# Order of the hand-over work between an expert mixture and a state-space layer, one power instruction, and squares made beside a sort

## The reference, cut to what matters

```python
# first mixture: top 2 of 8 experts, 256 hidden units
for e in range(n_experts):
    h = jax.nn.gelu(tokens @ w1[e].T, approximate=False)
    out = out + gate[:, e:e + 1] * (h @ w2[e].T)
...
# state-space layer, behind a layer norm and an RMS norm
u = h @ Win + b_in                       # 128 -> 256 channels
u = causal_conv(u, conv_w, taps=4) + conv_b
hc = einsum('bdr,drs->bds', hc, A) + u_t[:, :, None] * Bv[None]   # 16 states a channel, A is 16x16
y = einsum('bds,ds->bd', hc, Cv)
return y @ Wout + b_out + res
```

## Time and profile before

| | before |
|---|---|
| median of 3 runs | 1023.79 us (1021.31 to 1026.02) |
| the profiled execution, its own time | 1022.04 us |
| its span in the trace | 1020.2 us |
| mean granted clock of TensorE | 0.923 of 2.4 GHz |
| busy: PE / DVE / ACT / POOL | 867.4 / 540.7 / 453.2 / 462.6 us |
| attention with its sorts ends, first copy of the ticks | 380.06 us |
| tick 1 begins on PE | 390.23 us |
| squares of the last tick done, turning for the scan begins | 606.21 us |

### The profile page before, as it was taken

How to read it: one execution, slowest core, us unless ns; L and a number is a source line. 1 busy time by engine, 2 the same in 40 slices (tenths; PEclk the granted TensorE clock), 3 DMA queues, 4 the chain that set the end, 5 groups by cost and what they waited for, 6 DMA issues and landing times. The chain is left out here.

```text
span 1020.2 us, 25008 instructions
## 1 busy us (share of the span) xinstructions
PE 867.4 (85%) x9254; PEld 730.8 (72%) x9254; DVE 540.7 (53%) x1574; ACT 453.2 (44%) x991; POOL 462.6 (45%) x491
## 2 busy tenths in 40 slices
PE   4999999999998509977777469999977999999991
PEld 2777777777776508966666349999876679999991
DVE  4666657666576534444555557446376823222225
ACT  5545445454443004535554457442414453444443
POOL 3234353444444464655544410015503277677764
PEclk9999999999999758979888769999997999999995
DMA  7676700000000013322221110000014023322245
GB/s 251 232 282 266 300 23 8 13 16 8 18 13 17 22 45 83 106 75 74 65 66 28 42 21 4 3 4 2 1 31 180 17 73 80 88 81 89 86 114 165
DMA packets 72148, 78.78 MB, mean 77 GB/s; under 512 B 14285, under 2 KB 55892, under 8 KB 71536
## 3 DMA queue, kind: packets, MB, share of 16 engines
q1 hardware_dynamic: 61024, 59.02, 18.4%
q0 software_dynamic: 9152, 16.84, 4.8%
q10 hardware_dynamic: 1872, 1.58, 0.5%
HBM read 31.79 MB, written 47.64 MB: 78 GB/s over the span
## 5 line engine op out<-in xcount | busy, mean ns | idle before, releaser
L1733 POOL DMA_INDIRECT mixed<-ssm_H,ssm_target x78 | 77.4, 992 | 97.1 <-DVE ssm_H L2214 82.3
L449 POOL TENSOR_TENSOR attn_qd<-attn_qT,attn_qpow 128x512 f32<-128x512 f32 x32 | 51.3, 1602 | 130.5 <-DVE attn_qT L775 130.5
L1335 ACT ACTIVATE routed_hT<-routed_hid,routed_B 128x256 f32<-128x256 f32 x160 | 65.8, 471 | 81.0 <-PE routed_hid L1258 81.0
L1176 POOL DMA_INDIRECT results<-routed_outs,routed_target x80 | 78.5, 981 | 30.5 <-issue 16.5
L1161 POOL DMA_INDIRECT queue_in<-routed_XN,routed_slot x64 | 63.7, 995 | 45.3 <-DVE routed_slot L1436 22.3
L1270 PE MATMUL routed_outp<-routed_W,routed_hT 128*128 128x128 f32 x640 | 77.8, 275 | 0.0
L1258 PE MATMUL routed_hid<-routed_cols,routed_W 128*128 128x256 f32 x320 | 75.8, 380 | 0.5 <-DVE routed_cols L1484 0.5
L1270 PEld LDWEIGHTS routed_outp<-routed_W,routed_hT 128*128 128x128 f32 x640 | 74.7, 192 | 0.1
L439 POOL DMA_INDIRECT sorted_rows<-attn_sent_rows,attn_slot x56 | 57.2, 1022 | 18.3 <-issue 14.3
L1258 PEld LDWEIGHTS routed_hid<-routed_cols,routed_W 128*128 128x128 f32 x320 | 57.7, 190 | 6.9 <-ACT routed_shared L1314 0.7
L1824 PE MATMUL ssm_pb<-powers_XB,powers_XC 64*64 64x65 f32 (+4 forms) x640 | 31.8, 244 | 35.2 <-ACT powers_XC L2057 24.2
(11 more groups left out here) (339 smaller groups left out, 2263.1 us busy)
## 6 DMA issues: line engine op xcount, KB each, us to landing
sorted_rows<-attn_vacant SPq DMA_DIRECT2D x8, 2080.0 KB, 8.7
queue_in<-attn_empty SPq DMA_DIRECT2D x8, 645.0 KB, 7.2
routed_rows<-queue_in SPq DMA_DIRECT2D x40, 129.0 KB, 2.3
ssm_H<-sorted_rows SPq DMA_DIRECT2D x39, 130.0 KB, 2.1
results<-attn_zero SPq DMA_DIRECT2D x8, 512.0 KB, 8.2
ssm_turn_buf<-mixed SPq DMA_DIRECT2D x16, 256.0 KB, 3.3
routed_W<-m1w SPq DMA_DIRECT2D x2, 2048.0 KB, 10.2
xs<-x SPq DMA_DIRECT2D x8, 256.0 KB, 4.2
```

The source lines that it names most:

```text
L449: pool.tensor_tensor(wide(of_pair(qd, p)), wide(of_pair(qT, p)), qpow[:, p * P:(p + 1) * P].unsqueeze(1).to_broadcast([P, BATCH, P]), ALU. ...
L1176: pool.indirect_dma_start(results, bass.IndirectOffsetOnAxis(target[:, n:n + 1], 0), outs[t % KEPT_BACK][:, j * P:(j + 1) * P], None, boun ...
L1335: last = act.activation(hT[t % 2][:, m * GROUP:(m + 1) * GROUP], banks[q % 4][:, (m % 2) * GROUP:(m % 2 + 1) * GROUP], ACT.Silu, bias=B1[: ...
L1733: pool.indirect_dma_start(results, bass.IndirectOffsetOnAxis(target[:, 2 * q + j:2 * q + j + 1], 0), outs[q][:, j * P:(j + 1) * P], None, ...
```

## The change

**The tick table.** Every link of the hand-over chain gets a tick of its own, and some run at the start of a tick's body where they ran at its end:

| step | before | after |
|---|---|---|
| SP fetch back | 18, end | 17, end |
| POOL add (`mixed`) | 15, end | 14, end |
| DVE add and statistics (`mixed`, `stated`) | 16, end | 16, end |
| POOL powers | 16, end | 17, start |
| DVE shift (`scaled_means`) | 17, end | 18, start |
| ACT tokens | 17, end (ahead of the copies of squares) | 19, end |
| PE columns | 18, end | 20, start |
| PE input products | 19 and 20, end | 20 and 21, end |
| ACT columns, channels | 19; 20 and 21 | 20; 21 and 22 (ahead of the first weights) |
| DVE taps | 22, 23, 24 | 22, 23, 24 |

**One power.** Both variances stand side by side in one buffer, and POOL's two powers are one instruction of 128 x 2 x 4.

**The ring of rows.** It has 5 buffers (was 4). The tags are no longer copied: `kept_of` reads them from the rows, and a buffer is given back to SP only after it.

**The squares.** They move to a class that both phases use. 22 of the 40 sets are made at the end of the attention phase, in the banks of scores and products that are free by then, two pairs in turn: 5 sets ahead of the last chunk's `rows_turned`, 3 between its `logits_of` and `counted`, 14 behind `counted`. The other 18 follow on ticks 34 to 51, one a tick, with one pair of banks.

```diff
-            pool.tensor_tensor(of.both[:, tiles], of.wide_var[:, tiles], of.mhalf[:, tiles], ALU.pow)
-            front.power(pool, c, tiles)
+            pool.wait_ge(front.moments, at(c, 7, 7))
+            pool.tensor_tensor(of.pair(of.inverse, tiles), of.pair(of.spreads, tiles), of.pair(of.mhalves, tiles), ALU.pow
+                               ).then_inc(front.rstd_ready, 1)
...
+            def squares_kept(begin, end):
+                for m in range(begin, end):
+                    squares.kept(act, m, *squares_at(m))
...
             spread(LAST - 1)
+            squares_kept(0, SQUARED_FIRST[0])
             rows_of(LAST)
             sorted_columns(LAST)
+            squares_kept(SQUARED_FIRST[0], SQUARED_FIRST[1])
             spread(LAST)
+            squares_kept(SQUARED_FIRST[1], SQUARED_FIRST[2])
...
+            squares_of(0, SQUARED_FIRST[0])
             rows_turned(LAST)
             logits_of(LAST, proj[1])
+            squares_of(SQUARED_FIRST[0], SQUARED_FIRST[1])
             pe.wait_ge(s["put"], at(LAST - 1, PLACED, SUMS_READ))
             counted(LAST, proj[0])
+            squares_of(SQUARED_FIRST[1], SQUARED_FIRST[2])
...
+SQUARED_FIRST = (5, 8, 22)
...
-        FETCHED_BACK, MIXED, STATED, SCALED, TURNED, INPUT, KEPT_IN, CONVOLVED = 18, 15, 16, 17, 18, 19, 20, 22
+        FETCHED_BACK, MIXED, STATED, ROOTED, SCALED, TURNED, INPUT, CONVOLVED = 17, 14, 16, 17, 19, 20, 20, 22
...
+        LATE = TICKS - 1 - (NSQUARES - SQUARED_FIRST[-1])
...
             for t in range(TICKS):
+                if due(t, TURNED) is not None:
+                    columns(due(t, TURNED))
...
-                if t < NSQUARES:
-                    squares(t)
+                if squares_due(t) is not None:
+                    squares.multiplied(pe, squares_due(t), squares_b, squares_c, turns=1)
...
             def columns_of(n):
-                if n >= BODY:
-                    dve.wait_ge(s["outs"], n - 1)
                 dve.tensor_copy(cols[n % 2], turn).then_inc(s["cols"], 1)
-                dve.tensor_copy(tag4[:, n % BODY], by_row(rows[n % BODY])[:, :, D:TAGGED]).then_inc(s["rows_read"], 1)
...
                 kept.then_inc(s["outs"], 1)
+                dve.wait_ge(s["outs"], n + 3)
+                dve.sem_inc(s["rows_read"], 1)
```

More of the change, by code:

```diff
@@ L179, in attention_phase @@
                     queue, results, coming, sorting, table, sorted_rows, router, rank, before,
-                    powers):
+                    powers, squares):
     with ExitStack() as ctx:
@@ L619, in outputs_turned, with squares_of @@
                 mm.then_inc(s["ytr"], 1)
+            def squares_of(begin, end):
+                pe.wait_ge(s["zeroed"], 11)
+                for m in range(begin, end):
+                    squares.multiplied(pe, m, *squares_at(m), turns=2)
             def combined(i):
@@ L1591, in first_vectors, with __init__, multiplied, kept @@
             pool.tensor_copy(row[:, :, 0:1], table[:, :, STATES:STATES + 1])
-def mixed_space_phase(nc, xs, of, W1, W2, table, sorted_rows, powers, scratch, results):
+class Squares:
+    def __init__(self, S, powers):
+        self.b3, self.c3 = powers.b3, powers.c3
+        self.product, self.copied = (S.sem(n) for n in "product copied".split())
+    def multiplied(self, pe, m, bank_b, bank_c, turns):
+        k, q = divmod(m, NT)
+        n = 2 ** k
+        if m >= turns:
+            pe.wait_ge(self.copied, m - turns + 1)
+        for left, right, bank in ((self.c3, self.b3, bank_b), (self.b3, self.c3, bank_c)):
+            for k_, g in enumerate(range(SETS[q].start, SETS[q].stop)):
+                for part in ROWS:
+                    mm = pe.matmul(bank[part, k_ * (n + HALF):(k_ + 1) * (n + HALF)], left[part, g, n:n + HALF],
+                                   right[part, g, 0:n + HALF], start=True, stop=True)
+        mm.then_inc(self.product, 1)
+    def kept(self, act, m, bank_b, bank_c):
+        k, q = divmod(m, NT)
+        n = 2 ** k
+        act.wait_ge(self.product, m + 1)
+        act.activation(self.b3[:, SETS[q], n:2 * n + HALF], wide(bank_b[:, 0:SET * (n + HALF)], SET), ACT.Copy)
+        src = wide(bank_c[:, 0:SET * (n + HALF)], SET)
+        if k < LEVELS - 1:
+            act.activation(self.c3[:, SETS[q], n:2 * n + HALF], src, ACT.Copy).then_inc(self.copied, 1)
+        else:
+            act.activation(self.c3[:, SETS[q], n:2 * n], src[:, :, 0:n], ACT.Copy)
+            act.activation(self.c3[:, SETS[q], REACH + 1:REACH + 1 + HALF], src[:, :, n:n + HALF], ACT.Copy
+                           ).then_inc(self.copied, 1)
+SQUARED_FIRST = (5, 8, 22)
+def mixed_space_phase(nc, xs, of, W1, W2, table, sorted_rows, powers, squares, scratch, results):
     with ExitStack() as ctx:
@@ L1612, in lent @@
             return H[:, cut[0] - width:cut[0]]
-        rows = [lent(2 * TAGGED) for _ in range(BODY)]
+        rows = [lent(2 * TAGGED) for _ in range(RING)]
         cols, w1, w2 = ([lent(GROUP) for _ in range(2)] for _ in range(3))
@@ L1812, in output_of @@
                 mm.then_inc(s["outp"], 1)
[L1814 to L1820, removed]
-                for left, right, bank in ((c3, b3, squares_b), (b3, c3, squares_c)):
-                    for k_, g in enumerate(range(SETS[q].start, SETS[q].stop)):
-                        for part in ROWS:
-                            mm = pe.matmul(bank[part, k_ * (n + HALF):(k_ + 1) * (n + HALF)], left[part, g, n:n + HALF],
-                                           right[part, g, 0:n + HALF], start=True, stop=True)
-                mm.then_inc(s["lev_mm"], 1)
             def columns(i):
@@ L2318, in build @@
             sorting = Sorting(Scope(nc, until_spaced, "sorting"))
+            squares = Squares(Scope(nc, until_spaced, "squares"), powers)
             with ExitStack() as until_mixed:
```

101 lines of the change are left out of this document (48 added, 53 removed).

## The result

The changed kernel takes 969.94 us (968.15 to 974.8), against 1022.55 on the same chip; the ratio is 0.949, 95% interval 0.944 to 0.954. A second set of runs, beside the experiments, gave 974.09 against 1019.25: 0.954 (0.951 to 0.957).

What follows compares the result with a forecast made beforehand. PE bounds the ticks, standing 7.02 us in hand-over periods for ACT's copies of squares behind a POOL-DVE-ACT chain. From 1022.04, -1.3 + 17.4 + 28.3 + 5.5 - 16.6 = 33.3 saved: 989 us, range 972 to 1006.

Steps and rivals of the forecast that it cites:

- POOL sends at its floor: Ticks 1 to 13: POOL's two sends of 0.97, each behind 0.30 of issue, set 2.54 us a tick, 33.0 in all.
- the sort hides the 22 sets: Last sort: sets fit in PE's idle time at full clock; 1.3 us taken as cost, bounds -3 to +14.
- the periods: Ticks 18 to 33, four ticks with a hand-over each: 16.5 us a period, before 22.7; 28.3 saved in all.
- the price of the tail: From tick 39 on: 13 sets, PE and ACT in turns; 40 to some 58 us, 49 taken, 16.6 lost.
- ticks 34 to 38: Squares are back on these ticks: 5 x 3.2 + 2.9 + 3.8 = 22.7 us, before 28.2; 5.5 saved.
- wait of 3.8: PE's wait in a hand-over for DVE's tick of 6.0 us against PE's 2.12; also counted in ticks 34 to 38.
- Tags read from the rows save DVE a copy per tick: Ticks: tags uncopied, SP's buffer back two ticks later, fetch still two ticks ahead with five buffers; effect nothing.
- A: Rival, chance 0.22: hand-over wait stays and moves to PE's columns; periods 18.4 plus 1.8 per hand-over, 999 to 1000 us.
- B: Rival, chance 0.06: POOL's sends and powers exclude DVE's taps, adds and SBUF copies; periods 17.7, 995 us.
- C: Rival, chance 0.04: PE's gaps drop the ticks' clock to 0.50, 3.9 us a tick; slower, 1050 us.
- D: Rival, chance 0.04: all 14 sets in the sort's tail run at half clock, phase 13 us later; 1002 us.
- the term of 1.3: Last sort: three sets between logits and counting delay it, 0.5 us at full clock, 2.4 at half; 1.3 taken.

Runs made afterwards that it cites:

- e3: The changed kernel with POOL's two powers of 128x4 in place of the one of 128x8: 974.29 us, ratio to before 0.957.
- e7: The changed kernel with a second pair of banks for the squares in the tail, from tick 40 on: 972.88 us, ratio to before 0.955.
- e1: The changed kernel's hand-over order, one power and ring of five, but all 40 sets one per tick on ticks 0 to 39 as before: 980.13 us, ratio 0.961.
- e4: The changed kernel, but SP's fetch waits directly for the scaled outputs and DVE no longer waits for its own result: 961.4 us, ratio to before 0.942.
- e2: The kernel before with only the squares moved; hand-over ticks, two powers, ring and tags as before: 1002.2 us, ratio to before 0.983.
- e5: The changed kernel run again unaltered: 974.09 us, ratio to before 0.954.
- e6: The changed kernel with DVE's copies of the tags put back, ring of five kept, buffer given back with the copy: 961.68 us, ratio to before 0.943.
- e9: The kernel of e4 with both adds of a chunk on DVE: 959.77 us, ratio to before 0.940.

## Why the prediction was right and wrong

**The mechanism was right.** PE's wait for copies behind ACT's tokens is gone, POOL sends at its floor to tick 13 (forecast 33.0 for 13 ticks; POOL's own pace gives 2.55 a tick), the late link behind is DVE, the sort hides the 22 sets (its stage 35.3, forecast 36.2), and the periods are 15.6 to 17.1 (forecast 16.5).

**The step that failed is the price of the tail**, with that of ticks 34 to 38: forecast 71.8 for both, measured 59.6, with 55.1 to 59.6 in the other profiles that have the same order and the same squares there. That is 12 us of the 14.6 that are missing behind the attention. Cut where the forecast cuts, at the start of tick 39 (510.95), the tail took 42.3 for a forecast of 49, and ticks 34 to 38 took 17.3 for 22.7.

For the tail the forecast put the 13 sets and the three hand-overs in a row, 40 at full clock and some 58 at half (its terms as written add up to 55), and took the middle: 9 us for low clock. The 40 was near and the 9 was wrong. The granted clock was 0.92, with PE kept busy by the sets, against 0.63 in the earlier trace rows. Windows of PE alone that hold the tail and some us ahead of it, of the changed kernel and of e3:

```profile
505.00:553.00 48.00, 35.65 (x590) 0.93 0.08 24
```

```profile
512.00:560.00 48.00, 35.34 (x627) 1.00 0.09 24
```

The tail of e3 has the same order and the same sets, and PE waits in it as in the changed kernel (6.2 us for copies of squares, 2.4 for tokens in both). At 1.00 it took 40.6, against 43.5. So the low clock cost 2.9 and not 9; no run set the clock on purpose, e3 happened to keep it. The changed kernel pays it in one place, behind waits of 1.87 and 0.78, where the granted clock was 0.50 from 526 to 532 us; its timeline of PE:

```profile
525.13 0.66 PE L1887 MATMUL ssm_pb<-powers_ident,ssm_hn 128*128 128x128 f32 x4 [1.87 <-ACT ssm_hn L2107]
526.56 2.08 PE L1894 MATMUL ssm_pb<-ssm_hT,powers_WIN 128*128 128x512 f32 x2 [0.78 <-ACT ssm_hT L2115]
...
528.57 1.33 PE L1634 MATMUL ssm_pb<-powers_XB,powers_XC 64*64 64x80 f32 x16
...
532.80 0.77 PE L1634 MATMUL ssm_pb<-powers_XB,powers_XC 64*64 64x80 f32 x16
...
535.06 0.77 PE L1634 MATMUL ssm_pb<-powers_XB,powers_XC 64*64 64x80 f32 x16 [0.93 <-ACT powers_XC L1649]
```

The row of turns isn't the tail's only limit, which the forecast did not see. In e7 most of the turns are gone and the tail is 42.0; in e1 and before, with one set in it, it takes 34.8 to 36.9 by the chain of the last three hand-overs. So twelve more sets cost 2 to 9 there (39.0 to 43.5 in all), not 16.6. In ticks 34 to 38 the forecast's wait of 3.8 did not come: with a set in each tick PE waits for nothing there. And the last two ticks have no rows to turn, the last one no hidden units either, which the forecast priced in full.

That the 969.94 lies outside the range at all is chance on top of this: 6.3 us of the first profile's difference lie in the attention, and the second set of runs is inside.

**A part was costed wrong and didn't show.** "Tags read from the rows save DVE a copy per tick" and the ring were put at nothing or a gain. The diff shows the wait behind DVE's scaling; what stands behind it on DVE (the load for the weights' copy, then that copy, the taps, the statistics) was not counted. It costs 0.87 a tick, 3.5 a period of DVE's time, and 2.2 a period in the time of ticks 18 to 33 (e4). So it is luck in good part that the forecast of 16.5 for a period met the measured 15.6 to 17.1: without the wait that was not in the sum the periods are 13.0 to 15.7.

**The rivals.** A didn't happen: PE's columns never wait in the periods; e2 has the periods that A would have given, 18.3 to 19.5, though there PE waits for DVE's copies. B holds for the add and not for the power or the sends: a pair of taps beside the power of 474.92 took 1.41, and one beside the send of 463.49 took 1.41 too. C didn't: clock 1.00 in ticks 1 to 13 with PE busy 27.84 of 30.43 us. D didn't: the ticks' first copy came 26.6 behind the turning, 25.8 before. Timeline of the changed kernel, all engines, the end of the sort:

```profile
351.28 1.13 PE L1634 MATMUL attn_score<-powers_XB,powers_XC 64*64 64x65 f32 x16
...
354.81 0.79 PE L1634 MATMUL attn_score<-powers_XB,powers_XC 64*64 64x65 f32 x16
...
356.00 0.41 PE L602 MATMUL attn_proj<-attn_either,routing_before 128*128 128x32 f32 x2
...
374.60 0.42 ACT L2092 ACTIVATE ssm_H<-mixture_W 128x256 f32 x1 [3.60 <-PEq L1852]
```

Two of the three sets run at half clock (1.13) and the third near full (0.79), so the counting starts 8.0 behind the turning, 8.2 before: the term of 1.3 was, if anything, too high.

The other 6 us by which the profiled execution lies lower go with the attention's clock, in code that the change leaves alone (e5). What sets it is open; no run here varied it on purpose.

## What to carry to other kernels

When small work is moved to a stage in which an engine stood idle, don't price that stage at the clock that it had while idle. Here the tail's granted clock rose from 0.63 to 0.92 with the sets in it, and the sum at full clock (40) was near what came (39.0 to 43.5). Size the stage by its own chain as well: without the moved work it took 34.8 to 36.9.

Count every wait that a diff adds on an engine by what stands behind it in that engine's program. Here a saved copy of 0.17 us was paid with 0.87 us of idling, most of it a load that had run beside other work. Letting the consumer wait on the signal that exists already takes the idling away (e4: 5.8% under before, the change 4.6 to 5.1%), and so does the copy (e6: 5.7%). The fastest kernels here are e9, e4 and e6, not told apart in time.

## What the runs showed of the hardware

In these kernels DVE loads the address for a later instruction beside the work that runs, unless a wait that isn't met yet stands ahead of the load. With such a wait the load began 0.13 us behind the end of the scaling 37 times of 37, and DVE stood 0.86 to 0.88 us nearly each time (up to 1.01), in 35 ticks of the changed kernel; without it the load began 0.58 us or more ahead of that end (before and e4). The wait for DVE's own result alone cost 0.03 (e9). A DVE cast of 128x2 took 1.93 us beside POOL's add of 128x512 and 0.16 without it; DVE's taps beside POOL's power kept their 1.41 a pair.

The same stretch of attention was granted 0.68 to 1.00 of the clock from 320 to 340 us in thirteen executions, whose turning came up to 10 us apart. A single profile's time says little about a change of 1% here, while the stages behind it repeat to 0.4 us.
